# A graph layer with thirty feed-forward steps: two orders for VectorE and ScalarE by round, a variance on GpSimd, and a first stage shared out anew

## The chip, the core and the metric

The kernel runs on one core of a Trainium2 chip. The metric is the device time of the whole program in microseconds. Engines are named as in the profile: PE (TensorE, matrix products and transposes), DVE (VectorE), ACT (ScalarE), POOL (GpSimd), SP (SyncE, which here only starts DMAs).

## What is computed

12500 rows of 256 float32 numbers, 200000 weighted edges sorted by destination. From the reference, cut to what matters:

```python
xn = _layernorm(x, axis=-1)
x = x + _L0_gnn_ref(xn, edge_index, edge_weight, L0_gnn_weight) + _L0_mix_ref(xn[None], ...)[0]
x = x + _L0_ffn_ref(_layernorm(x, axis=-1)[None], L0_ffn_ln_w, L0_ffn_ln_b, L0_ffn_W, L0_ffn_b)[0]

# graph part: support = xn @ weight; agg = segment_sum(support[src] * edge_weight, dst); relu(agg)
# mix part: linear attention, sum over all rows of k'v, then q @ kv @ wo.T + bo
# feed-forward part, 30 steps on each row:
def step(h, _):
    h = h + 0.01 * jnp.tanh(h)
    h = h * jax.nn.sigmoid(h)
    h = _layernorm(h, ln_w, ln_b)
    h = jnp.einsum('bsc,dc->bsd', h, W) + b
    return (h, None)
```

Each row's statistics are its own; only the attention sum needs all rows.

## The kernel before

The rows are cut into 98 tiles of 128. The program has three stages.

*First stage (0 to about 100 us).* 24 groups of four rows per partition (`A_GROUPS`, `A_DEEP`) go through a ring of eight buffers `a_x`. SP loads a group (`a_load`, line 388; from the ninth on it waits for the store of the group eight before it). DVE makes statistics (line 963), variance plus epsilon `a_ve` (969) and, one group later, the shift `a_sh` (975). POOL raises the variance to the power -0.5 (`a_rs`, 517). ACT applies scale and shift, one operation for each of the four rows (`a_norm`, 650), and issues the store to `xn_d` (`a_store`, 656). Between groups ACT issues the loads of the weights: six large ones after group 0 (664), six small ones after group 1 (667 to 670) and eight small ones after group 2 (673 to 676). DVE also finds in this stage where each tile's edges begin, and prepares the weights. POOL's first gather waits until every group is stored.

*Second stage (about 100 to 652 us).* The attention sum over all tiles, and the graph part of the first 20 tiles: POOL gathers source rows from `xn_d` in chunks of 128 edges (`gather`, 534), 17 a tile, DVE makes a weighted one-hot matrix for each (`hot`, 1043), and PE multiplies the two into `AGG` (1310).

*Feed-forward rounds (652 us to the end).* Five rounds (`ROUNDS`) of 20 tiles (the first has 18). A round keeps its tiles in SBUF (`T`) for all 30 steps. Five quads of four tiles take turns; one quad in one step is a unit `n`. The engines run through the same list of slots `s`, 15 to a trip (three steps), ten trips to a round, each in its own function `f_trip` and with its own lag. In slot `n`:

- PE transposes unit n+1 into `TR` (`f_transpose`, line 1394), which has one buffer and so waits for `low_ready` of unit n, and then multiplies unit n (`f_multiply`, 1402): 24 products, since each factor is split in a high and a low part. Then come the chunks of the next tiles' graph part (`g_chunk`, 1310) and some small transposes and products into `XB` (1316, 1322).
- ACT copies `TR` into `v_high` for unit n+1 (`copy_t`, 752), normalises three of the four tiles of unit n+2 (`norm`, 743; two in the last round), takes SiLU of unit n+4 (`silu`, 738) and tanh of unit n+5 from the products of unit n (`tanh`, 728).
- DVE makes `v_low` of unit n+1 (`f_low`, 1169), one-hot matrices, the shift of unit n+3 (`f_shift`, 1140), the statistics and variance of unit n+4 (`f_stats`, 1130 and 1135) and the sum of unit n+5 (`f_sum`, 1155), which reads the products of unit n.
- POOL gathers (534), normalises the tiles of unit n+2 that ACT leaves (`f_norm`, 583), and raises the variance of unit n+3 to the power -0.5 (`f_rstd`, 517).

Rounds 0 to 3 (`xx` is true) prepare the next round's tiles in the same slots: gathers, chunks, `XB` work, and statistics of the new rows (1112 to 1124). The last round has only the feed-forward work. Each engine works through its list in the order in which it is written; semaphores say when a step is ready. The last five slots of a round also add the result to `x_cur` (`f_end`, 1177) and start the next round's units.

## Time and profile before

| | us |
|---|---|
| median of 3 runs | 4259.59 (4257.86 to 4260.25) |
| the profiled execution | 4259.98 |
| its span | 4257.9 |
| PE / DVE / ACT / POOL busy | 4002.0 / 3773.6 / 3431.0 / 3187.2 |
| rounds 1 and 2, each | 760 |
| last round | 598 |
| first stage | 100 |

The profile gives for each engine how long it was busy, which says little here, since four engines are busy for most of the span and the stages differ. Three views are used: busy time by stretch, waits by stretch, and the instructions in order of time. In the latter a row is start, duration, engine, line, operation, what is written and read, and how many instructions were merged; in brackets stands how long the engine was idle before it and what ended that.

### The profile page before, as it was taken

What the parts mean: (1) busy time and instruction counts of PE and PEld (TensorE: products, weight loads), DVE (VectorE), ACT (ScalarE), POOL (GpSimd) and SP (SyncE); (2) the same over time, 40 slices, a digit from 0 to 9 for tenths busy, and PEclk for the clock granted to TensorE, in tenths of its full rate; (3) what the DMA queues carried; (4) which work ended last, traced back from release to release, by engine and by line L of the source; (5) the groups of instructions that cost most, each with busy time, mean ns of one, the idle gap of its engine ahead of it and who ended that gap; (6) DMA issues with size and microseconds to landing.
All of it is one profiled execution on the core that took longest, in us unless ns stands there. A gap on an engine that the chain in (4) does not pass through costs nothing.

```text
span 4257.9 us, 83442 instructions
## 1 busy us (share of the span) xinstructions
PE 4002.0 (94%) x29048; PEld 3700.9 (87%) x29048; DVE 3773.6 (89%) x7327; ACT 3431.0 (81%) x5127; POOL 3187.2 (75%) x3679
## 2 busy tenths in 40 slices
PE   1789879999999999999999999999999999999999
PEld 0466668999998999999999999999999999899998
DVE  5577668989999999999999999999999999999998
ACT  5222237888888998989888899898998999999998
POOL 3666658888888888888888888888888886455554
PEclk9899989999999999999999999999999999999999
DMA  8444322222223222222232222223222221100000
GB/s 295 142 130 131 112 69 82 77 77 79 77 80 94 84 75 81 78 80 76 77 106 74 79 80 75 82 78 102 74 80 82 74 80 55 52 1 1 1 1 25
DMA packets 215400, 340.33 MB, mean 80 GB/s; under 512 B 79160, under 2 KB 152502, under 8 KB 214994
## 3 DMA queue, kind: packets, MB, share of 16 engines
q0 software_dynamic: 80768, 219.99, 17.8%
q1 hardware_dynamic: 118366, 82.88, 6.7%
q10 hardware_dynamic: 15860, 32.15, 2.2%
q8 instruction: 243, 3.98, 0.4%
q14 instruction: 163, 1.34, 0.1%
HBM read 298.20 MB, written 36.65 MB: 79 GB/s over the span
## 4 chain that ended last, share of the span: by engine, by line
PE 51%; DVE 26%; ACT 10%; POOL 5%; issue 5%; another core or an unknown queue 2%; DMA 1%; ACTq 0%; POOLq 0%; DVEq 0%; SPq 0%
PE MM L1402 24%; PE TR L1394 10%; PE AGG L1310 9%; DVE st L1130 7%; DVE v_low L1169 6%; DVE T L1155 6%; ACT T L743 3%; ACT v_high L752 3%; ACT T L738 3%; POOL gat_even L534 3%; PE XB L1322 2%; PE MM L1352 2%; DVE hot L1043 2%; DVE ve L1135 2%
## 5 line engine op out<-in xcount | busy, mean ns | idle before, releaser
L534 POOL DMA_INDIRECT gat_even<-xn_d,src_cur x1496 | 1499.8, 1003 | 437.6 <-issue 358.4
L1402 PE MATMUL MM<-w_high,v_high 128*128 128x256 f32 x5880 | 1722.2, 293 | 0.0
L1402 PE MATMUL MM<-w_low,v_high 128*128 128x256 f32 x5880 | 1660.6, 282 | 0.0
L1402 PE MATMUL MM<-w_high,v_low 128*128 128x256 f32 x5880 | 1659.5, 282 | 0.0
L1402 PEld LDWEIGHTS MM<-w_low,v_high 128*128 128x128 f32 x5880 | 1125.2, 191 | 0.0
L1402 PEld LDWEIGHTS MM<-w_high,v_high 128*128 128x128 f32 x5880 | 1122.5, 191 | 0.0
L1402 PEld LDWEIGHTS MM<-w_high,v_low 128*128 128x128 f32 x5880 | 1122.1, 191 | 0.0
L1130 DVE BATCH_NORM_STATS2 st<-T 128x6 f32<-128x512 f32 x1470 | 968.4, 699 | 146.3 <-ACT T L738 107.5
L743 ACT ACTIVATE T<-T,sh,rs 128x256 f32<-128x256 f32 x2042 | 1078.8, 592 | 0.5 <-DVE sh L1140 0.5
L752 ACT ACTIVATE v_high<-TR 128x1024 fp32r<-128x1024 f32 (+1 forms) x750 | 757.1, 1009 | 253.2 <-PE TR L1394 238.0
L1169 DVE SCALAR_TENSOR_TENSOR v_low<-TR,v_high 128x1024 fp32r<-128x1024 f32 (+1 forms) x750 | 895.5, 1194 | 31.9 <-ACT v_high L752 27.7
L517 POOL TENSOR_TENSOR rs<-ve,minus_half 128x4 f32<-128x4 f32 (+1 forms) x755 | 775.9, 1028 | 186.9 <-DVE ve L1135 183.8
L1155 DVE SCALAR_TENSOR_TENSOR T<-T,MM 128x1024 f32<-128x1024 f32 (+1 forms) x725 | 863.1, 1190 | 0.0
L1394 PE MATMUL TR<-ident,T 128*128 128x128 f32 x5916 | 781.0, 275 | 72.5 <-DVE v_low L1169 50.2
L1394 PEld LDWEIGHTS TR<-ident,T 128*128 128x128 f32 x5916 | 674.8, 141 | 174.9 <-DVE v_low L1169 114.7
L738 ACT ACTIVATE T<-T 128x1024 f32<-128x1024 f32 (+1 forms) x750 | 773.8, 1032 | 24.6 <-DVE T L1155 23.6
L1310 PE MATMUL AGG<-gat_even,hot 128*128 128x256 f32 x2992 | 755.2, 380 | 4.6 <-issue 3.7
L728 ACT ACTIVATE T<-MM 128x1024 f32<-128x1024 f32 (+1 forms) x725 | 719.3, 992 | 3.5 <-PE MM L1402 3.5
L583 POOL TENSOR_SCALAR T<-T,rs,sh 128x256 f32<-128x256 f32 x898 | 499.7, 560 | 233.7 <-DVE sh L1140 215.9
L1310 PEld LDWEIGHTS AGG<-gat_even,hot 128*128 128x128 f32 x2992 | 537.6, 191 | 81.1 <-issue 26.9
L1043 DVE TENSOR_SCALAR hot<-iota_f,d_loc,w_loc 128x128 f32<-128x128 f32 x1666 | 503.3, 352 | 0.8
L1135 DVE TENSOR_SCALAR ve<-st 128x4 f32<-128x4 f32 (+1 forms) x755 | 209.6, 278 | 25.9
(181 smaller groups left out, 2537.9 us busy)
## 6 DMA issues: line engine op xcount, KB each, us to landing
gat_even<-xn_d,src_cur POOLq DMA_INDIRECT x1496
a_x<-in_x SPq DMA_DIRECT2D x24, 512.0 KB, 6.7
xn_d<-a_x ACTq DMA_DIRECT2D x24, 512.0 KB, 5.0
out_rows<-x_cur SPq DMA_DIRECT2D x23, 512.0 KB
a_x<-xn_d ACTq DMA_DIRECT2D x20, 512.0 KB
x_n<-xn_d SPq DMA_DIRECT2D x80, 128.0 KB
x_d<-x SPq DMA_DIRECT2D x80, 128.0 KB
x_cur<-x_d SPq DMA_DIRECT2D x20, 512.0 KB
```

The lines of the kernel that those rows point to most:

```text
L517: pool.tensor_tensor(out_, var, minus_half[0:p, 0:n], ALU.pow).then_inc(S(done), 1)
L534: pool.indirect_dma_start(gat[gathered_in(j)][c][:], None, xn_d, bass.IndirectOffsetOnAxis(ap=src_cur[j % 2][:, c:c + 1], axis=0)).then_in ...
L728: nc.scalar.activation(lane(T, q, unit_tiles(n)), product(b, unit_tiles(n)), ACT.Tanh).then_inc(S("tanh_done"), 1)
L738: nc.scalar.activation(lane(T, q, unit_tiles(n)), lane(T, q, unit_tiles(n)), ACT.Silu).then_inc(S("silu_done"), 1)
L743: last = nc.scalar.activation(T[0:R, q * QT + t, :], T[0:R, q * QT + t, :], ACT.Identity, bias=sh[q][0:R, t:t + 1], scale=rs[q][0:R, t:t + 1])
L752: nc.scalar.activation(v_high[b][:, 0:banks], TR[:, 0:banks, 0:4 * R], ACT.Copy, bias=1.0).then_inc(S("transposed_copied"), 1)
L1130: last = v.bn_stats(st[q][0:R, t:t + 2].rearrange("p t k -> p (t k)"), rows_[:, t:t + 2, :].rearrange("p t f -> p f t"))
L1155: v.scalar_tensor_tensor(out=out_, in0=out_, scalar=0.01, in1=h, op0=ALU.mult, op1=ALU.add).then_inc(S("u_done"), 1)
L1169: v.scalar_tensor_tensor(out=v_low[b][:, 0:banks], in0=TR[:, 0:banks, 0:4 * R], scalar=1.0, in1=v_high[b][:, 0:banks], op0=ALU.add, op1=AL ...
L1310: mm(messages(j), hot[c][:], gat[gathered_in(j)][c][:], start=c == 0, stop=c == KC - 1).then_inc(S("chunks_multiplied"), 1)
L1394: last = tp(TR[:, t // 2, at:at + R], T[0:R, q * QT + t, h * 128:(h + 1) * 128], ident[0:R, 0:R])
L1402: last = mm(MM[b][0:R, t // 2, t % 2 * D:(t % 2 + 1) * D], rows_, w, start=k == 0, stop=k == len(products) - 1)
```

## The change

1. In rounds 0 to 3, ACT takes SiLU of unit n+3 at the head of slot n (before: of unit n+4 ahead of the tanh). DVE makes the statistics and variance of unit n+3 at the head of slot n and the shift of unit n+3 at its end. The last round keeps the order of before; its first slot has both, to pass from one to the other, and the second stage makes one unit less.
2. From unit 600 on, the units of the last round, POOL makes the variance, ahead of its power.
3. In the first stage the 14 small weight loads are issued by SP, ahead of its ninth group, and POOL normalises the last of a group's four rows, after the power of the next group. ACT's store and PE's reads of a group wait for both.

```diff
--- before.py
+++ after.py
@@ -30,6 +30,7 @@
+LAST_ROUND = (ROUNDS - 1) * TRIPS * SLOTS
@@ -392,6 +393,16 @@
             sp.dma_start(z_x[0:A_REST, 1, :], x[A_ROWS * 128:N, :]).then_inc(S("z_loaded"), 16)
+            for b in range(2):
+                sp.dma_start(lnw_c[:, b:b + 1], ln_w[b * 128:(b + 1) * 128].unsqueeze(1)).then_inc(S("weights_loaded"), 16)
+                sp.dma_start(lnb_c[:, b:b + 1], ln_b[b * 128:(b + 1) * 128].unsqueeze(1)).then_inc(S("weights_loaded"), 16)
+            sp.dma_start(c_row[:], bf.partition_broadcast(128)).then_inc(S("weights_loaded"), 16)
...
+                sp.dma_start(bv_col[b * HD:(b + 1) * HD, :], bv.unsqueeze(1)).then_inc(S("weights_loaded"), 16)
             for g in range(A_RING, A_GROUPS):
@@ -516,13 +527,22 @@
+            def a_norm(g):
+                b = g % A_RING
+                pool.wait_ge(S("a_shifts"), g + 1)
+                t = A_DEEP - 1
+                pool.tensor_scalar(a_x[b][:, t, :], a_x[b][:, t, :], a_rs[b][:, t:t + 1], a_sh[b][:, t:t + 1], ALU.mult, ALU.add).then_inc(S("a_normed_by_pool"), 1)
+
             for g in range(A_GROUPS):
                 rstd(a_rs[g % A_RING][:], a_ve[g % A_RING][:], A_DEEP, "a_variance", g + 1, "a_rstd", 128)
+                if g >= 1:
+                    a_norm(g - 1)
                 if g == FIND_AT:
...
+            a_norm(A_GROUPS - 1)
             rstd(z_rs[:], z_ve[:], 2, "a_variance", A_GROUPS + 1, "a_rstd", 128)
@@ -575,6 +595,9 @@
             def f_rstd(n, q):
                 tiles = unit_tiles(n)
+                if n >= LAST_ROUND:
+                    pool.wait_ge(S("stats"), n + 1)
+                    pool.tensor_scalar(ve[q][0:R], st[q][0:R, :, 2], 1.0 / D, EPS, ALU.mult, ALU.add).then_inc(S("variance"), 1)
                 rstd(rs[q][0:R, 0:tiles], ve[q][0:R, 0:tiles], tiles, "variance", n + 1, "rstd")
@@ -646,13 +669,14 @@
-                for t in range(A_DEEP):
+                for t in range(A_DEEP - 1):
...
             def a_store(g):
                 act.wait_ge(S("a_normed"), g + 1)
+                act.wait_ge(S("a_normed_by_pool"), g + 1)
@@ -662,18 +686,6 @@
-                if g == 1:
-                    for b in range(2):
-                        act.dma_start(lnw_c[:, b:b + 1], ln_w[b * 128:(b + 1) * 128].unsqueeze(1)).then_inc(S("weights_loaded"), 16)
...
-                if g == 2:
...
-                        act.dma_start(bv_col[b * HD:(b + 1) * HD, :], bv.unsqueeze(1)).then_inc(S("weights_loaded"), 16)
@@ -823,8 +835,6 @@
-                if s == START_STEP + 5:
-                    silu(3, 3)
@@ -836,6 +846,8 @@
                 for s in range(SLOTS):
                     n = t * SLOTS + s
+                    if xx or (u == 0 and s == 0):
+                        silu(n + 3, (s + 3) % QUADS)
@@ -852,7 +864,7 @@
-                    if not (last and s + 4 >= SLOTS):
+                    if not xx and not (last and s + 4 >= SLOTS):
                         silu(n + 4, (s + 4) % QUADS)
@@ -1157,7 +1169,8 @@
                 quad_stats(q, lane(T, q, unit_tiles(n)), unit_tiles(n), "stats")
-                quad_var(q, unit_tiles(n), "stats", n + 1, "variance")
+                if n < LAST_ROUND:
+                    quad_var(q, unit_tiles(n), "stats", n + 1, "variance")
@@ -1217,10 +1230,9 @@
-                for n in range(4):
+                for n in range(3):
                     if s == START_STEP + 3 + n:
                         f_stats(n, n)
@@ -1233,6 +1245,8 @@
+                    if xx or (u == 0 and s == 0):
+                        f_stats(n + 3, (s + 3) % QUADS)
                     if not (last and s + 1 >= SLOTS):
                         f_low(n + 1, 1 - b)
@@ -1256,9 +1270,9 @@
-                    if not (last and s + 3 >= SLOTS):
+                    if not xx and not (last and s + 3 >= SLOTS):
                         f_shift(n + 3, (s + 3) % QUADS)
-                    if not (last and s + 4 >= SLOTS):
+                    if not xx and not (last and s + 4 >= SLOTS):
                         f_stats(n + 4, (s + 4) % QUADS)
@@ -1267,6 +1281,8 @@
                         f_sum(n + QUADS, q, product(b, unit_tiles(n)))
+                    if xx:
+                        f_shift(n + 3, (s + 3) % QUADS)
@@ -1334,6 +1350,7 @@
                     pe.wait_ge(S("a_normed"), min(K_LOADS + k // A_DEEP, A_GROUPS) + 1)
+                    pe.wait_ge(S("a_normed_by_pool"), min(K_LOADS + k // A_DEEP + 1, A_GROUPS))
```

In a middle trip of rounds 0 to 3, one slot on DVE. Before it was (`T<-T,MM` is the sum, `hot` the one-hot matrices):

```order
L1169 SCALAR_TENSOR_TENSOR v_low<-TR,v_high 128x1024
L1043 TENSOR_SCALAR hot<-iota_f,d_loc,w_loc 128x128 x2
L1140 SCALAR_TENSOR_TENSOR sh<-st,rs 128x4
L1130 BN_STATS st<-T 128x6 x2
L1135 TENSOR_SCALAR ve<-st 128x4
L1155 SCALAR_TENSOR_TENSOR T<-T,MM 128x1024
```

Now, from the same point of the slot before on:

```order
L1167 SCALAR_TENSOR_TENSOR T<-T,MM 128x1024
L1152 SCALAR_TENSOR_TENSOR sh<-st,rs 128x4
L1142 BN_STATS st<-T 128x6 x2
L1147 TENSOR_SCALAR ve<-st 128x4
L1182 SCALAR_TENSOR_TENSOR v_low<-TR,v_high 128x1024
L1055 TENSOR_SCALAR hot<-iota_f,d_loc,w_loc 128x128 x2
```

The statistics and the variance now stand between the sum and `v_low`.

ACT at the same place, in a slot that also copies `XB`. Before:

```order
L752 ACTIVATE v_high<-TR 128x1024
L743 ACTIVATE T<-T,sh,rs 128x256 x3
L695 ACTIVATE xb_t<-XB 128x256
L738 ACTIVATE T<-T 128x1024
L728 ACTIVATE T<-MM 128x1024
```

Now:

```order
L750 ACTIVATE T<-T 128x1024
L764 ACTIVATE v_high<-TR 128x1024
L755 ACTIVATE T<-T,sh,rs 128x256 x3
L707 ACTIVATE xb_t<-XB 128x256
L740 ACTIVATE T<-MM 128x1024
```

SiLU (`T<-T`) has moved from ahead of the tanh (`T<-MM`) to behind it, at the head of the next slot.

The last round. DVE's slot before, up to the next `v_low`:

```order
L1169 SCALAR_TENSOR_TENSOR v_low<-TR,v_high 128x1024
L1140 SCALAR_TENSOR_TENSOR sh<-st,rs 128x4
L1130 BN_STATS st<-T 128x6 x2
L1135 TENSOR_SCALAR ve<-st 128x4
L1155 SCALAR_TENSOR_TENSOR T<-T,MM 128x1024
L1169 SCALAR_TENSOR_TENSOR v_low<-TR,v_high 128x1024
```

Now:

```order
L1182 SCALAR_TENSOR_TENSOR v_low<-TR,v_high 128x1024
L1152 SCALAR_TENSOR_TENSOR sh<-st,rs 128x4
L1142 BN_STATS st<-T 128x6 x2
L1167 SCALAR_TENSOR_TENSOR T<-T,MM 128x1024
L1182 SCALAR_TENSOR_TENSOR v_low<-TR,v_high 128x1024
```

and POOL, where round 3 passes into the last one:

```order
L606 TENSOR_SCALAR T<-T,rs,sh 128x256
L528 TENSOR_TENSOR rs<-ve,minus_half 128x4
L606 TENSOR_SCALAR T<-T,rs,sh 128x256
L600 TENSOR_SCALAR ve<-st 128x4
L528 TENSOR_TENSOR rs<-ve,minus_half 128x4
L606 TENSOR_SCALAR T<-T,rs,sh 128x256
```

The variance `ve` has left DVE's list and stands ahead of POOL's power.

## Rows read from the trace of the kernel before

**Rows 1.** Busy time by stretch (PE, PEld, DVE, ACT, POOL): round 1, last round

```profile
1379.00:2139.00 760.00, 754.87 (x5720) 720.72 (x5720) 712.98 (x1367) 682.52 (x1001) 638.40 (x721) 1.00 0.28 81
...
3651.00:4249.00 598.00, 575.39 (x4766) 559.24 (x4765) 562.14 (x890) 564.40 (x739) 309.79 (x443) 1.00 0.03 9
```

**Rows 2.** Waits in the last round: us in total, times, longest

```profile
PEld TR L1394 <- DVE v_low L1169: 35.0, 72, 0.5
```

**Rows 3.** Instructions by time, last round, about two slots of DVE, PE, ACT, POOL

```profile
3800.46 1.22 DVE L1169 SCALAR_TENSOR_TENSOR v_low<-TR,v_high 128x1024 fp32r<-128x1024 f32 x1
...
3801.73 1.09 PE L1394 MATMUL TR<-ident,T 128*128 128x128 f32 x8 [0.28 <-DVE v_low L1169]
...
3802.92 1.03 ACT L752 ACTIVATE v_high<-TR 128x1024 fp32r<-128x1024 f32 x1 [0.38 <-PE TR L1394]
3803.84 1.08 ACT L743 ACTIVATE T<-T,sh,rs 128x256 f32<-128x256 f32 x2
3804.82 1.04 ACT L738 ACTIVATE T<-T 128x1024 f32<-128x1024 f32 x1
3805.77 1.00 ACT L728 ACTIVATE T<-MM 128x1024 f32<-128x1024 f32 x1
...
3805.90 1.33 DVE L1130 BATCH_NORM_STATS2 st<-T 128x6 f32<-128x512 f32 x2 [0.39 <-ACT T L738]
3807.26 0.17 DVE L1135 TENSOR_SCALAR ve<-st 128x4 f32<-128x4 f32 x1
3807.34 1.21 DVE L1155 SCALAR_TENSOR_TENSOR T<-T,MM 128x1024 f32<-128x1024 f32 x1
3808.47 1.22 DVE L1169 SCALAR_TENSOR_TENSOR v_low<-TR,v_high 128x1024 fp32r<-128x1024 f32 x1
...
3803.27 1.01 POOL L517 TENSOR_TENSOR rs<-ve,minus_half 128x4 f32<-128x4 f32 x1 [0.33 <-DVE ve L1135]
```

**Rows 4.** By time in rounds 0 and 2; last, the page's group of line 1135

```profile
2741.46 1.04 PE L1394 MATMUL TR<-ident,T 128*128 128x128 f32 x8
...
2745.20 1.02 PE L1310 MATMUL AGG<-gat_even,hot 128*128 128x256 f32 x4
2746.06 1.04 PE L1394 MATMUL TR<-ident,T 128*128 128x128 f32 x8
...
2748.65 1.21 DVE L1169 SCALAR_TENSOR_TENSOR v_low<-TR,v_high 128x1024 fp32r<-128x1024 f32 x1
...
2824.12 1.21 DVE L1169 SCALAR_TENSOR_TENSOR v_low<-TR,v_high 128x1024 fp32r<-128x1024 f32 x1
...
1015.62 1.09 PE L1394 MATMUL TR<-ident,T 128*128 128x128 f32 x8 [0.98 <-DVE v_low L1169]
...
2722.77 0.56 DVE L1135 TENSOR_SCALAR ve<-st 128x4 f32<-128x4 f32 x1
...
2722.52 0.75 POOL L564 TENSOR_TENSOR g_agg<-g_c,g_u 128x256 f32<-128x256 f32 x1
...
L1135 DVE TENSOR_SCALAR ve<-st 128x4 f32<-128x4 f32 (+1 forms) x755 | 209.6, 278 | 25.9
```

**Rows 5.** First stage: by time, one piece of the chain, busy time by stretch

```profile
35.01 2.07 ACT L650 ACTIVATE a_x<-a_x,a_sh,a_rs 128x256 f32<-128x256 f32 x4 [7.01 <-issue]
...
79.12 2.07 ACT L650 ACTIVATE a_x<-a_x,a_sh,a_rs 128x256 f32<-128x256 f32 x4 [0.41 <-ACT a_x L650]
...
41.41 1.30 DVE L963 BATCH_NORM_STATS2 a_st<-a_x 128x6 f32<-128x512 f32 x2 [9.42 <-DMA a_x<-in_x]
...
100.69 1.04 POOL L534 DMA_INDIRECT gat_even<-xn_d,src_cur  x1 [12.40 <-DMA xn_d<-z_x]
...
28.02 12.28 DMA xn_d<-a_x
...
0.00:100.00 100.00, 6.22 (x16) 4.25 (x16) 59.43 (x155) 52.16 (x99) 30.99 (x40) 1.00 0.90 307
...
50.00:60.00 10.00, 1.01 (x4) 0.93 (x4) 9.48 (x25) 5.64 (x12) 2.01 (x2) 1.00 1.03 391
```

More of the change, by code:

```diff
@@ L1219, in _ @@
                         f_sum(n, n, lane(h_next, n, unit_tiles(n)))
-                for n in range(4):
+                for n in range(3):
                     if s == START_STEP + 3 + n:
                         f_stats(n, n)
-                for n in range(3):
                     if s == START_SHIFT + n:
```

12 lines of the change are left out of this document (5 added, 7 removed).

## Prediction, made before the changed kernel was timed

> **What bounds the kernel now.** I read the busy times by stretch first, then who waits for whom in a stretch, then the instructions of a few microseconds in order of time. Everything is measured against the profiled execution: 4259.98 us, of which 4257.9 us is the span; the median of the runs shown is 4259.59 us, 0.4 us away, so I use them as one. A slot is the time in which one unit (four row tiles) passes each engine; a trip has 15, a round 150.
>
> In the last round (3651 us on) the four busy times are level, PE 575, DVE 562 and ACT 564 of 598 us, while POOL has 310 [rows 1]. Such a level picture means a loop through several engines. The waits say which: PE's weight loads wait 35.0 us for DVE's `v_low`, in 72 of 150 slots [rows 2]. [rows 3] hold the loop. `v_low` starts at 3800.46 and ends 1.22 later; PE transposes at 3801.73 (1.09); ACT copies at 3802.92, normalises from 3803.84, takes SiLU at 3804.82 to 3805.86; DVE then makes statistics at 3805.90, variance 3807.26, the sum 3807.34 and `v_low` again at 3808.47. That is 8.01 us for two slots, 4.0 for one, times 150 the 598 us of the round. Nowhere in it is a member idle for more than 0.1 us.
>
> In rounds 1 to 3 PE sets the time. A slot with two gathered chunks lasts 4.60 (transposes at 2741.46 and 2746.06), of which 3.74 up to the first chunk at 2745.20 and 0.43 a chunk [rows 4]. A trip's 34 chunks, four pairs of attention or weight products at 0.86, and four pairs of small transposes at 0.22 (of the chunks' and transposes' kinds) give 15 x 3.74 + 14.6 + 3.4 + 0.9 = 75.0 us. The trip measures 2824.12 - 2748.65 = 75.5. So no order on DVE or ACT can win more than 0.5 us a trip there (the last trip of a round apart). In round 0, where every fifth unit is half as large, PE does wait, 0.98 us at 1015.62 [rows 4], about 2.6 us a trip.
>
> At the end of the first stage ACT is last. Its groups follow each other in 2.48 us (2.07 for four rows, 0.41 for the store's issue), eight of them from 76.64 on, and POOL's first gather has waited 12.40 us when the last store lands [rows 5].
>
> **The change part by part.** *Last round, variance to POOL.* In the loop, statistics start at 3805.90 and the sum at 3807.34: 1.44. The two statistics follow each other without a wait, their second part 0.63 after the first, so the sum can follow them about 1.25 after their start. It gains 0.19 per two slots, 0.095 per slot. Bounds: 0.08 per two slots (only the variance's own place in the queue, 3807.26 to 3807.34) and 0.28 (its mean duration over the page's group, [rows 4]). Over 150 slots: 14 us, from 6 to 21. Is anything right behind? ACT's own slot is 3.77 (its four operations start 0.92, 0.98, 0.95 and 0.92 apart), PE's 3.74 [rows 4], DVE's at most 3.62 after the change (8.01 less its wait of 0.39, halved, less 0.19). The new loop gives 3.91, still the longest, so all of the 0.095 counts. POOL's added operation is not in the trace. The nearest rows put it between 0.1 and 1.0 (its power operation on the same 128x4, [rows 3]); I take 0.4. Its cover: POOL's power ends at 3804.28; the shift that needs it stands just ahead of the statistics of 3805.90 and of their wait of 0.39, so at 3805.4, and 1.1 us is free. Even 1.0 is hidden. Cost nothing; without cover it would be its own length per slot.
>
> *Rounds 0 to 3, two orders.* SiLU moves behind the next tanh and to the head of ACT's slot; DVE makes statistics and variance ahead of `v_low`, and the shift last. The rstd gets some 3 us instead of about 1, so DVE's waits for it go, but they are not on the path. A new loop appears: products of PE, tanh, sum, shift, statistics, variance, `v_low`, transposes two slots on, products. By the starts and durations of [rows 3]: tanh can start 4.04 after its slot's transposes (3801.73, 3805.77) and takes 1.00, then 0.04, sum 1.13, shift 0.07, statistics and variance 1.44, `v_low` 1.22, 0.05: 9.0 us for two slots. PE needs 9.20 for two of the shortest and 10.0 on average, so the loop fits, with 0.2 to spare in the shortest pairs. These are three a trip (the pairs of slots 5-6, 8-9, 9-10). In slots 3 and 9 DVE also makes 0.75 us of statistics for the next round; followed by two short slots (9 and 10) that costs 0.2.
>
> The variance is now in a loop, and it is not always 0.17. At 2722.77 it took 0.56 and ended within 0.1 us of POOL's operation that began at 2722.52; over the page's group the mean is 278 ns [rows 4]. So a slot carries 0.1 of such stretch on average, much more now and then. The three tight pairs lose about 0.1 each. New stall 0.2 + 0.3 = 0.5 a trip against 0.4 to 0.5 now: 0 to +0.2. I take +3 us over the 30 trips of rounds 1 to 3, from -6 to +20. The Trainium skill (Advanced Engine Details and Errata, Mode Summary) says that the second SBUF port of the Vector engine is shared with GpSimd and that the two "will interfere/block eachother"; the row agrees. By that rule alone every variance that meets an operation on POOL waits for its end; what that makes here is rival 1, which is worked out from rows.
>
> In round 0 the wait behind a half unit comes from `v_low` standing behind the sum. In the new order it stands behind the variance, some 0.3 earlier; I take -2 us for ten trips, from -6 to +6. At a round's end DVE has one more operation in each of five slots and is the bound in both orders: 0. In the last trip of round 3, without chunks, the new loop (4.5 a slot) is worse than the old (4.0), but DVE's extra work there takes about as long: 0, give or take 3.
>
> *First stage.* ACT's tail: one row of four goes, 0.49 x 8 = 3.9 us. POOL takes it behind the next group's power (1.0 + 0.56 = 1.6 a group, less than ACT's 1.98), so the store does not wait for it. The 14 small loads leave ACT: they are why ACT sat idle for 7.01 us ahead of group 3 at 35.01 (and half of that ahead of group 2). The chain runs through the store of group 2 (28.02, 12.28 to land), and DVE waits 9.42 us for data at 41.41 [rows 5]. With ACT free this store goes 4.0 us earlier. SyncE had nothing to do then (its next load waits for a store), so there they cost the path nothing. But the DMA engines moved 391 GB/s at their best (50 to 60 us) and 307 on average over the stage [rows 5]; the stage's 30.7 MB in 92 us need 334. So only part of the 4.0 comes through. I take 2, sum 6 us, from 0 to 10. The 14 loads' queue behind eight large loads is the risk: nothing reads them before 60 us. Gathers start when the stage ends, so what follows shifts with it; its waits are irregular, which I carry as 4 us either way.
>
> **Sum.** -14 +3 -2 -6 = -19: 4260 - 19 = 4241 us.
>
> **The rivals.**
> 1. *Slower: the new loop catches on POOL.* In round 1 POOL is busy 638 of 760 us [rows 1] plus the gaps between gathers, so the variance often meets it. The place is the three tight pairs of slots a trip, 120 in all, and it decides from a mean stretch of 0.2. With a gather of 0.95 us met each time, each loses 0.7: 84 us; met half of the time, with half of it left, about 50 in all with the slots beside them. Then 4241 + 50 = 4291. For it: the row at 2722.77. Against: the average, 0.1, and that a POOL that waits for the variance isn't running. Chance 0.12.
> 2. *The first stage hands nothing on and the middle pays.* The DMA engines bound the stage or its gain is lost in the irregular stage behind it, and the orders cost 0.3 us a trip more: 4260 - 14 + 9 = 4255. Chance 0.18.
> 3. *The last round keeps its pace*: another loop, or the sum that follows no closer than now. Only 6 us there: 4249. Chance 0.10.
> 4. *More than forecast*: the stage gains 10, round 0 six, the last round 18: 4224. Chance 0.05.
>
> **How the numbers follow.** The forecast has 0.55, with its own range of 4228 to 4252. A measurement of this kernel tells 0.2% (8.5 us) from no change. Below 4251: the forecast, rival 4, and two thirds of rival 3: 0.67. Within 4251 to 4268: rival 2 and the rest of 3: 0.21. Above: rival 1, 0.12. The range reaches over rivals 2 and 3 and leaves most of rivals 1 and 4 out: 4226 to 4262.
>
> **What would show each step.** Last round: 586 or less from its first `v_low` to the end, `v_low` to `v_low` 7.8 over two slots, PE's wait for `v_low` near 20 us. If that is 598, step one is wrong. Rounds 1 to 3: trips of 75.3 to 75.8; over 76 means that the loop of 9.0 doesn't fit, and `v_low` would then start late behind a long variance. First stage: ACT's groups 1.98 apart, group 9's data before 41, first gather at 92 to 96 instead of 100.69. Wrong altogether if the trips of rounds 1 to 3 lengthen by 1 us, which is 30 us.

## The result, and the profile after

The changed kernel takes 4250.62 us (median of 13 runs, 4248.02 to 4255.98) where the kernel before, beside it, takes 4259.59 (4253.27 to 4263.88): ratio 0.9981, 95% interval 0.9973 to 0.9988. That is 9 us where 19 were forecast. The profiled execution was the slowest of its 13, 4255.98 us with a span of 4253.9; a second profile of the same kernel (*changed_again* below) has a span of 4250.9.

Where the time went is read best from six rows, the first `v_low` of each round and the last of all (DVE by time; start, duration, engine, line, operation). First of the kernel before, then of the changed one:

```profile
652.33 1.23 DVE L1169 SCALAR_TENSOR_TENSOR v_low<-TR,v_high 128x1024 fp32r<-128x1024 f32 x1 [3.77 <-ACT v_high L752]
...
1379.47 1.21 DVE L1169 SCALAR_TENSOR_TENSOR v_low<-TR,v_high 128x1024 fp32r<-128x1024 f32 x1
...
2138.82 1.21 DVE L1169 SCALAR_TENSOR_TENSOR v_low<-TR,v_high 128x1024 fp32r<-128x1024 f32 x1
...
2898.87 1.21 DVE L1169 SCALAR_TENSOR_TENSOR v_low<-TR,v_high 128x1024 fp32r<-128x1024 f32 x1
...
3651.28 1.22 DVE L1169 SCALAR_TENSOR_TENSOR v_low<-TR,v_high 128x1024 fp32r<-128x1024 f32 x1
...
4248.48 1.23 DVE L1169 SCALAR_TENSOR_TENSOR v_low<-TR,v_high 128x1024 fp32r<-128x1024 f32 x1 [0.70 <-ACT v_high L752]
```

```profile
647.00 1.23 DVE L1182 SCALAR_TENSOR_TENSOR v_low<-TR,v_high 128x1024 fp32r<-128x1024 f32 x1 [3.77 <-ACT v_high L764]
...
1383.75 1.22 DVE L1182 SCALAR_TENSOR_TENSOR v_low<-TR,v_high 128x1024 fp32r<-128x1024 f32 x1
...
2144.98 1.22 DVE L1182 SCALAR_TENSOR_TENSOR v_low<-TR,v_high 128x1024 fp32r<-128x1024 f32 x1
...
2907.27 1.22 DVE L1182 SCALAR_TENSOR_TENSOR v_low<-TR,v_high 128x1024 fp32r<-128x1024 f32 x1
...
3662.47 1.22 DVE L1182 SCALAR_TENSOR_TENSOR v_low<-TR,v_high 128x1024 fp32r<-128x1024 f32 x1
...
4244.49 1.23 DVE L1182 SCALAR_TENSOR_TENSOR v_low<-TR,v_high 128x1024 fp32r<-128x1024 f32 x1 [0.70 <-ACT v_high L764]
```

The differences give the account: up to the rounds -5.3 us (profiles of kernels with the same first stage differ by up to 10 us there, see the table below); round 0 **+9.6** (727.1 to 736.8); rounds 1 to 3 +1.9, +2.2, +2.8; the last round -15.2 (597.2 to 582.0). So the last round gained what was forecast, and the new order took 16.5 us back in rounds 0 to 3, more than half of it in round 0.

*Last round.* The busy times over it, against [rows 1], and PE's wait, against the 35.0 us of [rows 2]:

```profile
3662.47:4244.49 582.02, 580.54 (x4760) 558.62 (x4759) 542.50 (x742) 570.36 (x739) 340.23 (x592) 1.00 0.03 9
```

```profile
PEld TR L1411 <- DVE v_low L1182: 13.4, 72, 0.9
```

By time, against [rows 3]; POOL's new operation takes 0.20 us and the loop for two slots 7.82 (3799.92 to 3807.74) instead of 8.01:

```profile
3799.92 1.22 DVE L1182 SCALAR_TENSOR_TENSOR v_low<-TR,v_high 128x1024 fp32r<-128x1024 f32 x1
...
3807.74 1.22 DVE L1182 SCALAR_TENSOR_TENSOR v_low<-TR,v_high 128x1024 fp32r<-128x1024 f32 x1
...
3802.89 0.20 POOL L600 TENSOR_SCALAR ve<-st 128x4 f32<-128x4 f32 x1 [0.48 <-DVE st L1142]
```

*Round 0*, behind a half unit. Units are counted here by their `v_low` in a trip, 0 to 14; in round 0 units 4, 9 and 14 are half as large. The kernel before, at units 10 and 11 (PE and DVE by time):

```profile
1063.64 1.06 PE L1394 MATMUL TR<-ident,T 128*128 128x128 f32 x8 [1.17 <-ACT T L743]
...
1060.34 1.21 DVE L1155 SCALAR_TENSOR_TENSOR T<-T,MM 128x1024 f32<-128x1024 f32 x1
1061.86 1.23 DVE L1169 SCALAR_TENSOR_TENSOR v_low<-TR,v_high 128x1024 fp32r<-128x1024 f32 x1 [0.31 <-issue]
...
1066.94 1.21 DVE L1169 SCALAR_TENSOR_TENSOR v_low<-TR,v_high 128x1024 fp32r<-128x1024 f32 x1
```

The changed kernel at the same place (PE, DVE, ACT, POOL):

```profile
1063.92 1.09 PE L1411 MATMUL TR<-ident,T 128*128 128x128 f32 x8 [1.36 <-DVE v_low L1182]
...
1069.27 1.09 PE L1411 MATMUL TR<-ident,T 128*128 128x128 f32 x8 [0.53 <-DVE v_low L1182]
...
1059.64 1.22 DVE L1167 SCALAR_TENSOR_TENSOR T<-T,MM 128x1024 f32<-128x1024 f32 x1 [0.59 <-issue]
...
1060.85 1.32 DVE L1142 BATCH_NORM_STATS2 st<-T 128x6 f32<-128x512 f32 x2
1062.20 0.55 DVE L1147 TENSOR_SCALAR ve<-st 128x4 f32<-128x4 f32 x1
1062.66 1.21 DVE L1182 SCALAR_TENSOR_TENSOR v_low<-TR,v_high 128x1024 fp32r<-128x1024 f32 x1
...
1067.08 1.02 DVE L1147 TENSOR_SCALAR ve<-st 128x4 f32<-128x4 f32 x1
1068.00 1.21 DVE L1182 SCALAR_TENSOR_TENSOR v_low<-TR,v_high 128x1024 fp32r<-128x1024 f32 x1
...
1058.58 1.02 ACT L740 ACTIVATE T<-MM 128x1024 f32<-128x1024 f32 x1 [0.74 <-PE MM L1419]
...
1061.80 0.95 POOL L554 DMA_INDIRECT gat_even<-xn_d,src_cur  x1 [0.30 <-issue]
...
1066.91 0.74 POOL L584 TENSOR_TENSOR g_agg<-g_c,g_u 128x256 f32<-128x256 f32 x1
1067.60 0.58 POOL L528 TENSOR_TENSOR x_rs<-x_ve,minus_half 128x1 f32<-128x1 f32 x1
```

Before, `v_low` followed the sum and ended at 1063.09, half a microsecond ahead of the transposes, which waited for ACT's normalisation. Now the sum is followed by shift, statistics and a variance of 0.55 us that ends with POOL's gather, and `v_low` starts 3.0 us behind the sum's start instead of 1.5: it is what PE waits for. One slot on, another variance takes 1.02 us, until POOL's two operations are about done, and PE waits a second time, where it had not waited before. Between the two `v_low`s DVE is never idle for more than 0.04 us. Over 600 us of round 0 (groups of instructions from 700 to 1300 us; the last field is the idle time before them and what ended it), before and after:

```profile
L1394 PE MATMUL TR<-ident,T 128*128 128x128 f32 x892 | 119.0, 274 | 18.3 <-ACT T L743 10.7 <-DVE v_low L1169 7.5
...
L1135 DVE TENSOR_SCALAR ve<-st 128x4 f32<-128x4 f32 (+1 forms) x124 | 34.2, 276 | 4.3
```

```profile
L1411 PE MATMUL TR<-ident,T 128*128 128x128 f32 x880 | 118.0, 275 | 25.0 <-DVE v_low L1182 24.1
...
L1147 DVE TENSOR_SCALAR ve<-st 128x4 f32<-128x4 f32 (+1 forms) x123 | 50.6, 411 | 4.2
```

*First stage.* ACT's groups of three, DVE's long wait, SyncE's loads and the first gather, against [rows 5]; the last row is the piece of the chain:

```profile
91.33 1.58 ACT L673 ACTIVATE a_x<-a_x,a_sh,a_rs 128x256 f32<-128x256 f32 x3 [0.40 <-ACT a_x L673]
...
42.67 1.30 DVE L975 BATCH_NORM_STATS2 a_st<-a_x 128x6 f32<-128x512 f32 x2 [10.81 <-DMA a_x<-in_x]
...
23.07 1.47 SPq L405 DMA_DIRECT2D bv_col<-in_bv  x1
24.58 18.64 SPq L389 DMA_DIRECT2D a_x<-in_x  x4
...
97.55 1.09 POOL L554 DMA_INDIRECT gat_even<-xn_d,src_cur  x1 [7.30 <-DMA xn_d<-z_x]
...
24.69 13.49 DMA xn_d<-a_x
```

The groups are 1.98 apart, as forecast, and the first gather is 3.1 us earlier, but DVE's long wait for data is 10.81 us instead of 9.42. Both numbers vary from profile to profile: in the fifteen profiles with this first stage the first gather comes at 96.5 to 98.1 us (median 97.1) and the long wait is 9.65 to 11.36; in the two with the old one (before and *pool_var_only*) they are 100.69 and 101.11, 9.42 and 9.55.

### The profile page after: what moved, and what is told of

Same layout as the page of the kernel before. It is cut to its first block, busy times and chain, and to the rows that moved or that the text cites. A ratio compares the mean times of both kernels' runs of the same rounds, so it can differ in the third digit from the quotient of the medians.

```text
span 4253.9 us, 83466 instructions
## 1 busy us (share of the span) xinstructions
PE 4012.3 (94%) x29048; PEld 3701.6 (87%) x29048; DVE 3786.8 (89%) x7177; ACT 3447.9 (81%) x5103; POOL 3234.0 (76%) x3853
## 3 DMA queue, kind: packets, MB, share of 16 engines
q14 instruction: 165, 1.35, 0.1%
## 4 chain that ended last, share of the span: by engine, by line
PE 73%; DVE 18%; ACT 3%; issue 3%; another core or an unknown queue 2%; DMA 1%; ACTq 0%; POOL 0%; DVEq 0%; SPq 0%
PE MM L1419 41%; PE TR L1411 13%; PE AGG L1326 11%; DVE st L1142 4%; DVE T L1167 4%; DVE v_low L1182 4%; PE XB L1338 3%; PE MM L1369 3%; DVE hot L1055 1%; ACT T L740 1%; PE XB L1332 1%; DVE ve L1147 1%; PE TR L1326 1%; DVE sh L1152 1%
## 5 line engine op out<-in xcount | busy, mean ns | idle before, releaser
L1055 DVE TENSOR_SCALAR hot<-iota_f,d_loc,w_loc 128x128 f32<-128x128 f32 x1666 | 494.6, 346 | 0.8
L554 POOL DMA_INDIRECT gat_odd<-xn_d,src_cur x170 | 169.7, 998 | 77.0 <-issue 38.4
```

The lines of the kernel that those rows point to most:

```text
L554: pool.indirect_dma_start(gat[gathered_in(j)][c][:], None, xn_d, bass.IndirectOffsetOnAxis(ap=src_cur[j % 2][:, c:c + 1], axis=0)).then_in ...
```

## The experiments

All in one table: ratio to the kernel before run beside them, with its 95% interval, and from each profile the first `v_low` and the length of the rounds in us.

| | ratio (interval) | first | 0 | 1 | 2 | 3 | last |
|---|---|---|---|---|---|---|---|
| before | | 652.3 | 727.1 | 759.4 | 760.1 | 752.4 | 597.2 |
| changed | 0.9981 (0.9973, 0.9988) | 647.0 | 736.8 | 761.2 | 762.3 | 755.2 | 582.0 |
| changed_again | 0.9974 (0.9964, 0.9984) | 645.4 | 737.2 | 760.8 | 761.8 | 754.4 | 582.1 |
| old_order * | 0.9958 (0.9945, 0.9972) | 560.7 | 725.5 | 760.0 | 759.5 | 752.0 | 582.2 |
| old_order_2 | 0.9957 (0.9943, 0.9970) | 638.5 | 727.4 | 759.1 | 760.3 | 752.7 | 582.2 |
| round0_old_order * | 0.9955 (0.9941, 0.9968) | 559.1 | 726.2 | 759.6 | 759.1 | 751.9 | 582.0 |
| round0_old_order_2 | 0.9973 (0.9962, 0.9983) | 646.3 | 727.3 | 763.2 | 761.1 | 754.7 | 582.1 |
| no_variance | 0.9921 (0.9907, 0.9934) | 637.6 | 730.3 | 757.4 | 756.7 | 749.2 | 582.0 |
| variance_twice | 1.0073 (1.0060, 1.0087) | 645.8 | 748.7 | 769.7 | 770.1 | 762.7 | 581.9 |
| var_behind_low * | 1.0110 (1.0094, 1.0125) | 557.9 | 752.3 | 772.4 | 773.7 | 764.8 | 582.1 |
| pool_var_all_rounds | 1.0359 (1.0345, 1.0374) | 646.0 | 788.0 | 795.8 | 799.5 | 785.6 | 582.1 |
| var_unstretched * | 0.9973 (0.9962, 0.9985) | 559.6 | 732.6 | 759.5 | 760.7 | 753.2 | 582.0 |
| x_stats_behind | 0.9992 (0.9983, 1.0001) | 645.9 | 743.4 | 758.8 | 759.5 | 753.4 | 582.0 |
| pool_var_only | 0.9960 (0.9946, 0.9973) | 649.8 | 726.7 | 760.4 | 759.5 | 752.6 | 582.1 |
| first_stage_only | 0.9996 (0.9986, 1.0005) | 640.8 | 729.2 | 760.7 | 760.3 | 753.4 | 597.3 |
| order_in_last_trips | 0.9953 (0.9940, 0.9967) | 641.2 | 727.1 | 758.0 | 758.9 | 751.6 | 582.1 |
| order_last_trips_2 | 0.9953 (0.9939, 0.9966) | 647.6 | 726.1 | 760.3 | 759.2 | 751.8 | 582.0 |
| loads_spread | 0.9946 (0.9932, 0.9959) | 639.6 | 726.9 | 760.2 | 758.3 | 751.4 | 582.0 |
| row_alone | 0.9945 (0.9931, 0.9959) | 645.5 | 727.4 | 758.0 | 759.0 | 752.0 | 582.0 |

\* on a chip on which the kernel before took 4170.2 us (see the last section). Lengths of the rounds repeat to within 1 to 2 us, round 0 less well: in the old order it is 725.5 to 729.2 in seven profiles. What lies ahead of the first `v_low` differs by up to 10 us between profiles of kernels whose first stages end alike, so the totals carry that much noise.

**Is it the order?** *old_order* is the changed kernel with the old order in rounds 0 to 3, *round0_old_order* with it in round 0 alone:

```
+NEW_ORDER = ()              # round0_old_order: (1, 2, 3)
...
-if xx or (u == 0 and s == 0):
+new = r in NEW_ORDER
+was = r - 1 in NEW_ORDER if r else 0 in NEW_ORDER
+if (new and not (u == 0 and s == 0 and not was)) or (not new and was and u == 0 and s == 0):
     f_stats(n + 3, (s + 3) % QUADS)
...
-if not xx and not (last and s + 4 >= SLOTS):
+if not new and not (last and s + 4 >= SLOTS):
     f_stats(n + 4, (s + 4) % QUADS)
```

(SiLU and the shift likewise.)

> The change without its new order: rounds 0 to 3 run in the order of before, POOL still makes the last round's variance and the first stage is the changed one. Theory A (the order itself costs the time of rounds 0 to 3, by statistics and variance in front of v_low): round 0 falls from 736.8 back to about 727 us and rounds 1 to 3 from 761.2, 762.3, 755.2 to 759.4, 760.1, 752.4; in total 4250.6 - 9.6 - 6.9 = about 4234 us, faster than both kernels. Theory B (round 0 is longer because of what the changed first stage hands it, earlier gathers and another phase of POOL): round 0 stays near 737 and the total falls by the 7 us of rounds 1 to 3 only, to about 4244.

> Round 0 alone in the order of before, rounds 1 to 3 in the new one. Theory A: round 0 back to 727, rounds 1 to 3 at 761 to 762, total about 4241 us, which is what was forecast. Theory B: round 0 stays at 737, total 4250.

Round 0 is back at 725.5 and 726.2 us, so theory A holds and B, the first stage's doing, falls. But the changed kernel itself was never run on this chip, and rounds 1 to 3 were no longer on it in the new order (trips of 75.60 us) than in the old. So the kernels ran again where the kernel before takes 4253 to 4260 us.

> The changed kernel itself, unaltered, beside the single parts on one chip (on the chip of the first four experiments the kernel before took 4170 us, 90 less than at first, all of it ahead of the rounds, so totals are compared as differences to before). If the effect is the same everywhere: 8 to 9 us less than before, round 0 at 736.8, rounds 1 to 3 at 761.2, 762.3, 755.2. If the trips of 75.6 that rounds 1 to 3 showed with round 0 in the old order are a matter of the chip and not of the code, they appear here too and this kernel is some 4 to 7 us further below before.

> Again the change without its new order, now beside the other parts, since the first time it ran on a chip on which the second stage took 90 us less. By the sum of the parts: last round -15, first stage -5, rounds as before: 4259.5 - 20 = about 4239 us, 9 to 16 us less than the changed kernel. If on this chip it comes out within 3 us of the changed kernel, the order costs nothing there and theory A falls.

> Round 0 in the old order, rounds 1 to 3 in the new, on this chip. If it is the code (the new order starts from the old one's lags and finds another rhythm against POOL): trips of 75.6 in rounds 1 to 3, total about that of the kernel with the old order everywhere. If it was the chip: trips of 75.9 to 76.0 as in the changed kernel, 5 to 7 us more than with the old order everywhere.

Here rounds 1 to 3 together take 2271.8 to 2274.4 us in the four profiles with the old order (before, *old_order_2*, *pool_var_only*, *first_stage_only*) and 2276.9 to 2279.0 in the three with the new one (*changed*, *changed_again*, *round0_old_order_2*), most of whose trips last 75.7 to 76.0: the order costs them 3 to 7 us. On the other chip it cost them nothing (2270.7 against 2271.5). Round 0 is at 727.4 and 727.3 again with the old order, against 737.2. The order moves SiLU on ACT as well as statistics, variance and shift on DVE; no run takes the two apart. Old order everywhere: 4232.34 us, 4252.91 before beside it.

**What in the order?** The expectations below number the candidates: A1, the variance that now stands ahead of `v_low`, above all where POOL stretches it; A2, DVE's queue between two `v_low`s, too full by its plain length, mainly by the statistics; A3, a sum that comes late and holds up the next tanh. The kernel of *no_variance* leaves out the scaling by 1/D and the epsilon, so it computes something else and serves for its time alone.

```
 # no_variance, POOL, rounds 0 to 3 (DVE makes no variance)
-rstd(rs[q], ve[q], "variance", n + 1)
+rstd(rs[q], st[q][0:R, 0:tiles, 2], "stats", n + 1)
 # variance_twice, DVE
+quad_var(q, unit_tiles(n), "stats", n + 1, "variance_once")
 quad_var(q, unit_tiles(n), "stats", n + 1, "variance")
```

> The changed kernel with its order, and no engine makes the variance in rounds 0 to 3: POOL's power reads the statistics' sum of squares itself, so the scaling by 1/D and the addition of EPS are left out there. POOL's work stays what it was. Theory A1 (the variance, plain and stretched, in front of v_low costs round 0 its 9.6 us): round 0 at 726 to 729, below the 727 of the old order, and slot 11's stall of 0.64 us gone. Theory A2 (the 1.33 us of statistics that now stand in front of v_low fill DVE's queue behind the half units): slot 11's stall falls by the 0.3 us of a mean variance only, round 0 at 733 to 735. Rounds 1 to 3: 75.6 a trip by both.

> The changed kernel, in which DVE makes each variance of rounds 0 to 3 twice, one behind the other, the second for nothing. Theory A1a (the plain length counts wherever PE waits for v_low, slots 0, 5, 10 and 11 of round 0): each of them gets 0.12 to 0.17 us more, 0.5 us a trip, round 0 from 737 to 742, rounds 1 to 3 +0.15 a trip, in all +8 to +12 us. Theory A1b (mainly the stretch by POOL's operations costs, and the first variance has waited it out): the same small plain price, but where POOL's next operation follows at once the second copy is stretched as well and the price is far above 0.17: over 1 us a trip, total +25 us or more. Rival (the plain length has slack): below +3 us.

Without the variance, round 0 falls by 6.9 us to 730.3, between the two expectations (726 to 729, 733 to 735) and nearer to A1; its trips 1 to 8 last 72.3 to 72.5 us as in the old order (72.3), against 73.2 to 73.7. Of the remaining 3 us, 2 stand in the first and last trips (73.8 and 77.0 against 72.7 and 76.0 in the kernel before). Rounds 1 to 3 fall by 3 to 5 us each, below those of the old order. In all the variance costs rounds 0 to 3 in the new order 20.4 us (3014.0 less 2993.6). The same groups of instructions as above, without variance and with two:

```profile
L1414 PE MATMUL TR<-ident,T 128*128 128x128 f32 x892 | 119.0, 274 | 17.8 <-POOL T L609 11.6 <-DVE v_low L1185 6.2
```

```profile
L1414 PE MATMUL TR<-ident,T 128*128 128x128 f32 x872 | 117.3, 275 | 33.2 <-DVE v_low L1185 33.2
...
L1147 DVE TENSOR_SCALAR ve<-st 128x4 f32<-128x4 f32 (+1 forms) x242 | 78.1, 323 | 8.8 <-issue 0.3 <-DVE ve L1147 0.3
```

PE's wait follows the variance: 17.8, 25.0, 33.2 us. But without it two thirds of the wait are for POOL's normalisation and no longer for `v_low`. By unit, the mean wait of PE ahead of the transposes, over trips 1 to 8 of round 0, worked out from PE's rows (the gap to the product before, less 0.22), and the mean length of the variance just ahead of that unit's `v_low`:

| unit | 0 | 5 | 10 | 11 | sum |
|---|---|---|---|---|---|
| before, wait | 1.10 | 0.15 | 1.35 | 0.01 | 2.6 |
| changed, wait | 1.27 | 0.27 | 1.52 | 0.64 | 3.7 |
| its variance | 0.48 | 0.32 | 0.55 | 0.98 | |
| no_variance, wait | 0.85 | 0.00 | 0.93 | 0.82 | 2.6 |
| variance_twice, wait | 1.53 | 0.55 | 1.73 | 0.89 | 4.7 |

At units 0, 5 and 10 taking the variance away gives back 0.42, 0.27 and 0.59, about its whole length there, plain and stretched (0.48, 0.32, 0.55). Of these 1.35 us, 3 x 0.17 = 0.5 are plain, so the stretch is the larger part. Where PE doesn't wait for `v_low`, the length costs nothing: at unit 3 the variance takes 1.02 us, the longest mean of all, and PE's wait is 0.00 with it and without.

At unit 11 the wait stays, against both expectations, but it is another wait. In the changed kernel PE starts 0.06 us behind the end of `v_low`; in *no_variance* `v_low` ends 1.25 us ahead of the transposes, and PE waits for POOL, whose normalisation (1054.64 to 1055.37 at this place) stands behind two gathers and two operations for the next round:

```profile
1055.51 1.06 PE L1414 MATMUL TR<-ident,T 128*128 128x128 f32 x8 [0.69 <-POOL T L609]
```

So the variance's 0.98 did hold up `v_low` there, and another limit lies right behind it. At unit 0, too, PE waits for POOL in *no_variance*.

*variance_twice* costs 37 us in rounds 0 to 3 and 1.15 a trip in round 0, which is what A1b named (25 or more, over 1 a trip). Its reason doesn't fit as well: the price at each of the four places is 0.21 to 0.28, not far above 0.17, since the second variance takes 0.23 in the mean (78.1 less 50.6 us over 121). In rounds 1 to 3 it costs 0.9 a trip where A1a had 0.15; there PE's wait at unit 11 grows from 0.69 to 1.12, and `v_low` becomes what PE waits for at unit 10 too.

*var_behind_low* leaves the statistics ahead and makes the variance behind `v_low`; *pool_var_all_rounds* gives it to POOL everywhere:

```
 # var_behind_low, DVE
 f_stats(n + 3)            # without the variance
 f_low(n + 1)
+f_var(n + 3)
 # pool_var_all_rounds, POOL
-if n >= LAST_ROUND:
+if n >= 3:
     pool.tensor_scalar(ve[q], st[q][..., 2], 1.0 / D, EPS, ALU.mult, ALU.add)
```

> The changed kernel, but in rounds 0 to 3 DVE makes the variance behind v_low instead of in front of it; the statistics stay in front. Theory A1 (stretch): v_low no longer waits for a stretched variance, trips of round 0 fall from 73.3 to about 72.5 us and those of rounds 1 to 3 from 75.97 to about 75.6; total about 4239. Theory A2 (plain length): only 0.17 us of the loop goes, that is 3 stalls of 0.17 a trip at most, 0.3 to 0.5 us a trip in round 0, total about 4246. Against both: the rstd comes 1.2 us later and the shift at the slot's end could wait for POOL, which would give back some of it.

> The changed kernel with its order, and POOL makes the variance in rounds 0 to 3 too, so that only the statistics stand in front of v_low. Theory A1 (the variance in front of v_low, 0.17 us and stretched to 1.0 where POOL is in an operation, costs round 0 its time): round 0 back to 728 to 730 us and trips of rounds 1 to 3 at 75.6. Theory A2 (DVE's queue between two v_lows is full behind the half unit, mainly by the statistics): round 0 at 734 or more. Against both: POOL is busy 638 of 760 us in round 1 and gets 0.2 us a unit and a wait for the statistics more, which can delay its gathers; then trips above 76.

Both are far slower, by 46 and 152 us than the kernel before, where A1 and A2 both had them level with the changed kernel or faster, if nothing else got in the way. PE's waits in 700 to 1300 us, first with the variance behind, then with POOL's (in POOL's also DVE's shift):

```profile
PE TR L1416 <- POOL T L606: 34.0, 33, 2.1
```

```profile
PE TR L1411 <- POOL T L606: 46.8, 52, 2.2
DVE sh L1152 <- POOL rs L528: 31.0, 51, 1.2
```

The wait has moved to POOL's normalisation. That is the chain variance, power, shift, normalisation, transposes, and in rounds 0 to 3 POOL's gathers stand in it: what shortens `v_low`'s side lengthens this one. In the last round, without gathers, the same edit on POOL gains 15 us.

```
 # var_unstretched, DVE
-v.tensor_scalar(ve, st[..., 2], 1.0 / D, EPS, ALU.mult, ALU.add)
+v.scalar_tensor_tensor(out=ve, in0=st[..., 2], scalar=1.0 / D, in1=eps_col, op0=ALU.mult, op1=ALU.add)
```

> The changed kernel with its order kept; only DVE's variance in rounds 0 to 3 is another instruction that computes the same, a scalar_tensor_tensor with the constant from a column, as the shift is. The shift's median in the trace is 0.155 us and 51 of 755 are long, against 183 of 605 long variances. Theory A1 (the variance in front of v_low is stretched by POOL's operations, and that stretch is what the PE waits for): mean variance falls from 0.30 to about 0.19 us, stalls behind half units shrink by up to 0.5 us in slot 11, round 0 falls by 5 us or more, rounds 1 to 3 by 2 each, total about 4240. Theory A2 (the loop through statistics, variance and v_low is too long behind a half unit by its plain length): the stretch had slack, round 0 within 2 us of 737, total about 4249.

This tells nothing between A1 and A2, since the edit did not do what it was made for (and its round 0 of 732.6 has no changed kernel beside it on that chip). Its durations (minimum, median, maximum in ns) are as stretched as the old form's:

```profile
L1147 DVE SCALAR_TENSOR_TENSOR ve<-st,eps_col x605: 160/164/1037, 508.8 to 3551.1; 128x4 f32<-128x4 f32 x144, 128x2 f32<-128x2 f32 x8
```

*x_stats_behind* moves DVE's 0.75 us for the next round's rows from ahead of the sum to behind the shift.

> The changed kernel with DVE's statistics for the next round's rows (0.75 us, in slots 3 and 9) behind the sum and the shift instead of in front of the sum. They end up between the same two v_lows, so if DVE's queue as a whole is full there (theory A2), slot 11's stall of 0.65 us more stays, round 0 stays at 736 to 737. If the stall comes because the sum is late and the tanh of the next unit waits for it (theory A3), slot 11's stall goes: 0.5 us a trip in rounds 0 to 3, round 0 near 731, total 15 to 20 us less than the changed kernel.

A3 falls for round 0: the wait at unit 11 stays (0.60), and the one at unit 5 grows from 0.26 to 0.83; round 0 is 6 us longer, which neither expectation had. In rounds 1 to 3 it gains 5.2 us (unit 11's wait 0.69 to 0.45), where A3 expected such a gain. So at unit 11 in round 0 DVE's queue is full between two `v_low`s, as A2 has it, but by the variance of 0.98 and not mainly by the statistics, as *no_variance* shows.

**The last round alone.** *pool_var_only* is the kernel before with POOL's variance in the last round.

> The kernel before with one edit: POOL makes the last round's variance. Theory: it alone is the 15.2 us between the two traces' last rounds: last round 582 instead of 597, all else as before, total 15 us below before. Rival (part of the last round's gain was the order of the rounds before it or the phase in which they leave the units): less than 12.

582.1 instead of 597.2 and nothing else: the 15 us are this edit. At 4242.62 us against 4259.48 it alone beats the whole change.

**The first stage.**

> The kernel before with the changed first stage alone (small loads on SyncE's queue, one row of four normalised by POOL). Theory: the first v_low of the rounds comes 4 to 6 us earlier than in the kernel before (649.8 to 652.3 there, 645.4 and 647.0 in the two profiles of the change), the rounds stay at 727, 760, 760, 752 and the last at 597; total 4 to 6 us less, on the edge of what can be told. Rival (the gain of the first stage is lost in the second, and the earlier start in the two traces has another cause): within 1 us of before.

The first gather comes at 97.38 instead of 100.69. The total, 4250.84 against 4252.91, lies between the two expectations and can't be told from no change.

```
 # loads_spread, SyncE
-all 14 small loads ahead of the first reload
+two of them behind each of the first seven reloads
 # row_alone: the 14 back on ACT's queue, as before
```

> As the kernel with the new order in last trips only, but SyncE issues the 14 small loads in pairs, each behind one of the first seven reloads, instead of all ahead of them. Theory C (the small loads stand in front of the first reload and move it behind ACT's stores): the first reload is issued at about 23.5 when its store lands and lands before 32, DVE's long wait at 42 us falls from 10.8 to 8 or less, first gather at 94 to 96 instead of 97 to 98, the rounds 2 us earlier. Rival D (the DMA engines are full in these 50 us, 0.95 to 0.98 of their time, so the order of the transfers changes nothing of their sum): first gather still at 97 to 98.

> As the same base, but the 14 small loads are back on ACT's queue behind its second and third group, as in the kernel before; POOL still normalises one row of four. Theory C: ACT sits idle again for 7 us there, the first reload is issued at 22 to 23; the tail of ACT's groups, 0.49 x 8 = 3.9 us, is won all the same: first gather at 96.5 to 97.5, no later than with the loads on SyncE. Rival (moving the loads is what brought the 3.1 us): first gather at 99 or later.

> The base of the two again: POOL makes the last round's variance, the first stage is the changed one, and the new order stands only in the last trip of rounds 0 to 3. 17 to 21 us below the kernel before, first gather at 97 to 98.

In *loads_spread*, SyncE's first reload, DVE's long wait and the first gather; in *row_alone*, DVE's long wait and the first gather:

```profile
22.74 0.35 SPq L389 DMA_DIRECT2D a_x<-in_x  x1
...
39.65 1.30 DVE L976 BATCH_NORM_STATS2 a_st<-a_x 128x6 f32<-128x512 f32 x2 [6.75 <-DMA a_x<-in_x]
...
96.05 1.09 POOL L552 DMA_INDIRECT gat_even<-xn_d,src_cur  x1 [7.29 <-DMA xn_d<-z_x]
```

```profile
41.23 1.30 DVE L980 BATCH_NORM_STATS2 a_st<-a_x 128x6 f32<-128x512 f32 x2 [8.20 <-DMA a_x<-in_x]
...
94.46 1.09 POOL L544 DMA_INDIRECT gat_even<-xn_d,src_cur  x1 [7.27 <-DMA xn_d<-z_x]
```

(In the changed kernel the reload's row at 24.58 merges four reloads; the first landed at 42.65.) Spread, the first reload lands 7.3 us after its issue, at 30.0, instead of at 41.1 to 42.8 in the fifteen profiles with all the loads ahead of it, and DVE waits 6.75 instead of 9.65 to 11.36. That much of theory C holds. At the first gather little is left of it: 96.05, where the fifteen have 96.5 to 98.1. With the loads left on ACT it is better still: 94.46, or 6.2 us before the old 100.69 and 2 us earlier than expected. Moving the loads to SyncE cost 2 to 3.6 us at the first gather and did not bring any.

**A faster version.** *order_in_last_trips* has the new order only in the last trip of rounds 0 to 3 (`new = xx and end`).

> As the run beside it, with the new order only in the last trip of each of rounds 0 to 3, where the trace of the change shows 75.1 to 75.5 instead of 76.0, 78.5 to 78.9 instead of 79.7 twice and 71.5 instead of 73.0 us. Theory: the new order pays where DVE has the round's last sums to make and PE is not ahead: 0.6 + 0.9 + 0.9 + 1.3 = 3.7 us less than the kernel with the old order in all rounds, about 4235 us. Rival (these trips are short because the trips ahead of them ran in the new order and left other lags between the engines): no difference.

Rounds 0 to 3 take 2995.6 us against 2999.5 in *old_order_2*, 3.9 where 3.7 were expected; 2.4 of it stands in the four last trips themselves. The four profiles that have this order lie at 2995.6 to 2997.3; the four with the old order throughout on these chips at 2999.0 to 3003.6. The totals (4231.90 and 4232.34) do not tell them apart. The largest gains over the kernel before are those of *row_alone* (4235.05) and *loads_spread* (4235.28), where the kernel before took 4257.19: 22 us less, against 9 to 11 of the change. That they beat *order_in_last_trips* and *old_order_2* (21 us each) is not shown, as the intervals overlap.

## Why the prediction was wrong

- **Last round, -14: right.** -15.2, shown alone by *pool_var_only*; loop 7.82, the value forecast; POOL's operation 0.20, inside its bounds of 0.1 to 1.0; PE's wait 13.4 instead of the 20 expected.
- **Rounds 1 to 3, +3 (-6 to +20): right in kind, too small.** +6.9. Most trips last 75.7 to 76.0, at the edge of "over 76 means it doesn't fit", and 75.55 without the variance. The text priced the stretch at 0.1 in each of three pairs of slots; PE's wait sits at one unit, 11, behind the slot with the next round's statistics, and went from 0.34 to 0.72, about 10 us in the 27 trips ahead of the last ones.
- **The last trip of each round, 0: a term mis-sized.** The last trips of rounds 0 to 3 became 0.6, 0.8, 0.8 and 1.4 us shorter, 3.6 in all, and hid as much of the loss in the other trips.
- **Round 0, -2 (-6 to +6): the step that failed.** +9.6, outside its bounds. The text said that the wait behind a half unit comes from `v_low` standing behind the sum and that behind the variance it would stand "some 0.3 earlier". Three things were wrong with it. The row at 1015.62 [rows 4] is one of the waits for `v_low`, but over the round PE waited longer for ACT's normalisation (10.7 us against 7.5, at unit 10, where `v_low` ended 0.50 ahead of the transposes): moving `v_low` can't lift that. And "behind the variance" is behind sum, shift, statistics and variance, and the sum gains little by having nothing ahead of it, since it can't start before tanh: DVE idles 0.59 us ahead of the sum of 1059.64, as tanh ends at 1059.60. From the sum's start that is 3.0 us instead of 1.5, not 0.3 less. Last, the text had worked out the new loop at 9.0 us for two slots but held it only against PE's 9.20 for two full slots. Worked out from PE's rows, less its waits, PE needs 7.8, 8.9 and 7.3 us for the two slots that end at units 0, 5 and 10 of round 0; they took 8.9, 9.0 and 8.7 before and take 9.1, 9.1 and 8.8 now. A loop of 9.0 could gain nothing there. The stretch, known from 2722.77 [rows 4], then falls on just the places where PE waits: 0.48, 0.55 and 0.98 us where the mean before was 0.28. *no_variance* shows what the variance is worth: with it gone, trips 1 to 8 last 72.4 us, with it 73.4, in the kernel before 72.3.
- **First stage, -6 (0 to 10): inside its range, its steps wrong.** The first gather came 3.1 us earlier, at 97.55 and outside the 92 to 96 of the text; in total *first_stage_only* gained 2.1 us, which can't be told from none. The row on POOL alone is worth 6.2 at the first gather, not 3.9; "they cost the path nothing", of the loads on SyncE, was wrong by 2 to 3.6. They kept SyncE busy to 24.54 us, a microsecond past the landing of the store (23.45) that the first reload waits for. That the reload, issued this late, then queued behind ACT's stores is likely and was not tried by itself.
- **Rivals.** Rival 1 had the right mechanism, a `v_low` behind a variance that POOL stretches, at 50 us and in the wrong place (tight pairs of slots rather than behind half units); *no_variance* puts the whole variance at 20. Rival 2 (4255) came nearest for the rounds: it had the orders cost 0.3 us a trip more, and 16.5 us over 40 trips are 0.4. By the rule that the prediction took from the Trainium skill (Advanced Engine Details and Errata, Mode Summary) every variance that meets an operation on POOL would wait for its end. The trace bears that out in part: all 183 long variances of the changed kernel meet one, but of the 265 that start while one runs on, 111 stay within 1.5 times the median of 0.17 us. And a long one must stand where PE waits to cost anything.
- The parts add up to the profile: 4260 - 5 + 10 + 7 - 15 = 4257, rounded, against 4256. The median is 4251; the 5 us between are spread among executions of one kernel.

## What to carry to other kernels

Ahead of moving an operation into the path, list what stands between its new place and the instruction that has to wait anyway (here tanh): all of that counts. A mean wait is not one cause: ask per unit what ended it, since the places with another limit gain nothing and can lose. Hold a new loop against the shortest work in every stage, not in one of them. And a queue is only free if its last issue ends before the event for which its next one waits.

## What the runs showed of the hardware

- A 128x4 variance on DVE takes 0.17 us, or is stretched beside POOL's operations (to 1.07 us at most in the changed kernel): 183 of 605 are over 1.5 times the median, each meets an operation on POOL, and 118 of them end within 0.1 us of the end of one. The shift, which reads two SBUF tiles, is stretched too (51 of 755, up to 0.80 us), and so is the variance as a two-input operation (161 of 605). `v_low` and the sums of the trips, one of whose inputs lies in PSUM, never are (at most 1.233 and 1.224 us). For `v_low`:

```profile
L1182 DVE SCALAR_TENSOR_TENSOR v_low<-TR,v_high x750: 675/1217/1233, 647.0 to 4244.5; 128x1024 fp32r<-128x1024 f32 x180, 128x512 fp32r<-128x512 f32 x8
```

  The Trainium skill (SBUF — State Buffer, Who interferes with whom) says that a DVE instruction with two SBUF inputs contends with a GpSimd instruction that reads SBUF; the shift, the two-input variance and `v_low` agree with it, and by it *var_unstretched* could not have worked.
- The same program takes 2% less on another chip, all of it ahead of the rounds: the first `v_low` comes at 557.9 to 560.7 us instead of 637.6 to 652.3. From 200 to 400 us PE is busy 181.72 us in the changed kernel and 200.00 in *old_order* on that chip:

```profile
200.00:400.00 200.00, 181.72 (x766) 124.67 (x766) 142.75 (x345) 54.88 (x143) 133.44 (x136) 0.97 0.46 134
```

```profile
200.00:400.00 200.00, 200.00 (x884) 140.72 (x883) 166.24 (x399) 68.55 (x165) 151.96 (x157) 1.00 0.51 154
```

  What delays the stage on the one chip was not tried, and it stays open why the new order costs nothing in rounds 1 to 3 on the other.
